# Moving the low half of x from POOL to DVE in the first stage of an attention and feed-forward kernel

## The chip, the cores and the metric

One core of one Trainium2 chip. The metric is the time of one execution on the device in microseconds, as the median of several runs. The kernel before takes 1428.94 us.

## What is computed

A layer with attention and a gated feed-forward part side by side, on x of 4 x 1024 x 512 in float32. The reference, cut to what matters:

```python
xn = (x - mean(x)) / sqrt(var(x) + 1e-5)
q, k, v = (heads(xn @ W.T) for W in (Wq, Wk, Wv))     # 16 heads of 32
scores = where(causal, q @ k.T / sqrt(32), lowest)
attn = softmax(scores) @ v
gate = silu((xn @ fp8(gate_w)) * gate_scale)
up = (xn @ fp8(up_w)) * up_scale
ffn = ((gate * up) @ fp8(down_w)) * down_scale
out = x + attn @ Wo.T + ffn
```

## The kernel before

The kernel has two stages. `prepare` normalises x, makes q, k and v and stores them to DRAM; `attend` does the attention and the feed-forward part and reads them back. Products are made in float16 with a high and a low part for each float32 operand: high x high, high x low, low x high.

`prepare` goes over x in eight tiles of 512 rows, t = 0 to 7. A tile has twelve chunks, c = 0 to 11: four of q, four of k, four of v. TensorE makes a chunk in twelve matmuls of 128x512 (L797) into one of four banks; ScalarE copies the high part out as float16 (L487 for q and k, L491 for v), DVE subtracts it from the bank for the low part (L695, L699), and SP stores the pair (L386, L396). TensorE may begin chunk c when DVE has made the low part of chunk c - 4, since they share a bank. The float16 pairs of q and k stand in four buffers, so ScalarE's high part of chunk c also waits until the store of chunk c - 4 has landed.

While the chunks of tile t go by, the engines also make ready tile t + 1, each at a fixed place in its own hand-written order. In tiles 2 to 6 that is:

- DVE: statistics of x behind chunk 0 (L512, L516), the factor 1/sqrt(var) behind chunk 1 (L522 to L530), `normalise` behind chunk 2 (L537, x_in to xn).
- ScalarE: `x_high` behind chunk 4 (L450): the high half of xn as float16, into `x_part`.
- POOL: `x_low` (L429): xn less its high half, 128x2048, into the low half of `x_part`. POOL waits for `x_high` and for TensorE to be done with the former low half. Tile 0 has its low half from DVE (`first_x_low`, L594) instead.
- TensorE: `turn_x` behind chunk 9: 32 transposes (L737), in four fills, two of the high and two of the low half.
- ScalarE and DVE: `copy_x` behind chunk 10 (L469, L588): the turned halves into `x_t`. TensorE begins the next tile when both are done.

DVE has one more duty: rounding a piece of the feed-forward weights to fp8 in float32, three times a tile (`round_weights`, L616 to L632: maximum, mask of the exponent into `cmag`, L622 which clips `cmag`, L624 which adds it to `raw`, and the last step). In tiles 2 to 5 the three stand behind chunks 4, 6 and 8, in tile 6 behind 4, 6 and 9. Tile 0 and tile 1 also bring in the weights Wk, Wv and Wo: `weights_low` (L578) makes a low part of 128x2048 on DVE, `turn_weights` turns them on TensorE, `copy_weights` (L455, L544) takes them out. Tile 0 rounds behind chunks 7, 8 and 9; tile 1 has `weights_low(3)` and a rounding behind chunk 5, then further ones behind 7 and 8. Tile 0 makes `x_high` behind chunk 7.

In tiles 6 and 7 TensorE also makes scores of the first heads (L171), for whose row maxima DVE reduces the banks (`row_maxima`, L194, L199) behind chunks 3 to 8. Turning x in tile 6 waits for the twelfth of these reductions.

SP issues, once DVE's low part of chunk 11 is there, in this order: the store of v (L396), three loads of feed-forward weights (L339, L342), two stores of turned x (L367), then the stores of q and k as they come. Where DVE's order is decided:

```python
first_tile = {..., 6: ("normalise",), 7: ("round 0",), 8: ("round 1",), 9: ("round 2",)}
second_tile = {0: ("statistics",), 1: ("factor",), 2: ("normalise", "max 3"), 4: ("power 3",),
               5: ("low 3", "round 0"), 7: ("round 1",), 8: ("round 2",)}
other_tile = {0: ("statistics",), 1: ("factor",), 2: ("normalise",), 4: ("round 0",),
              6: ("round 1",), 8: ("round 2",)}
```

Of the kernel before, what the change touches and what calls it, by code (L numbers as in the profile page):

```python
# [18 lines left out]
ALU = mybir.AluOpType  # L19
# [12 lines left out]
NT = B * S // TILE  # L32
# [4 lines left out]
HI, LO = 0, 1  # L37
# [97 lines left out]
def wait(eng, sem, value):  # L135

    if value > 0:
        eng.wait_ge(sem, value)
# [72 lines left out]
def low_maxima(nc, pool, rows, m, par):  # L211

    pool.wait_ge(rows.m_red, NM * (m + 1))
    nc.gpsimd.tensor_scalar(rows.m_neg[:, :], rows.mx[par][:, :], -1.0 / MSCALE, None, ALU.mult).then_inc(rows.m_neg_set, 1)
    pool.wait_ge(rows.m_neg_set, m + 1)
    pool.wait_ge(rows.m_hi, m + 1)
    nc.gpsimd.tensor_tensor(rows.m_part[:, 8:16], rows.m_neg[:, :], rows.m_part[:, 0:8],
                            ALU.subtract).then_inc(rows.m_lo, 1)
# [15 lines left out]
def prepare(nc, x, weights, ffn, scales, xn_dram, keep, rows, bank):  # L234
# [11 lines left out]
    with ExitStack() as ctx:  # L246
        def sb(name, shape, dt):
            return ctx.enter_context(nc.sbuf_tensor(name, shape, dt))

        def sem(name):  # L250
            return ctx.enter_context(nc.semaphore(name))
# [10 lines left out]
        xn = sb("xn", [P, NB, D], F32)  # L262
        x_part = sb("x_part", [P, 2, NB, D], F16)
# [38 lines left out]
        xhi_done = sem("xhi_done")  # L302
        xlo_done = sem("xlo_done")
        xt_mm = sem("xt_mm")
# [24 lines left out]
        def has_next(t):  # L329
            return t < NT - 1  # L330
# [78 lines left out]
        @block.gpsimd  # L409
        def _(pool):  # L410
            nc.gpsimd.memset(ones[:, :], 1.0).then_inc(ones_ready, 1)
            nc.gpsimd.memset(ident[:, :], 0.0).then_inc(ident_zero, 1)
            pool.wait_ge(ident_zero, 1)
            nc.gpsimd.affine_select(out=ident[:, :], in_=ident[:, :], compare_op=ALU.not_equal, fill=1.0, base=0,
                                    pattern=[[-1, P]], channel_multiplier=1).then_inc(ident_set, 1)
            nc.gpsimd.memset(v_st[:, :, :, 2 * DK:VE], 1.0).then_inc(ones_set, 1)
            nc.gpsimd.memset(rows.mask[:, :], 0.0).then_inc(mask_zero, 1)
            pool.wait_ge(mask_zero, 1)

            nc.gpsimd.affine_select(out=rows.mask[:, 512 - P:512], in_=rows.mask[:, 512 - P:512],  # L420
                                    compare_op=ALU.is_ge, fill=MASKED, base=0, pattern=[[-1, P]],
                                    channel_multiplier=1).then_inc(mask_set, 1)

            def x_low(t):

                pool.wait_ge(xhi_done, t + 1)

                wait(pool, xt_mm, 4 * t)
                nc.gpsimd.tensor_tensor(x_part[:, LO, :, :], xn[:, :, :], x_part[:, HI, :, :],  # L429
                                        ALU.subtract).then_inc(xlo_done, 1)  # L430

            for t in range(1, NT):
                x_low(t)
            low_maxima(nc, pool, rows, 0, 0)

        def wmax_bank(m):
# [66 lines left out]
        def _(dve):  # L503
# [63 lines left out]
            def weights_power(m):  # L567

                at = slice(m, m + 1)
                dve.wait_ge(wmax_mm, m + 1)  # L570
                nc.vector.tensor_reduce(w_max[:, at], wmax_bank(m), AX.X, ALU.max).then_inc(wpow_set, 1)
                dve.wait_ge(wpow_set, m + 1)
                nc.vector.tensor_copy(w_pow[:, at], w_max[:, at])
                nc.vector.reciprocal(w_inv[:, at], w_max[:, at]).then_inc(winv_done, 1)
# [14 lines left out]

            for k_rows in rows.k_st:  # L590
                nc.vector.memset(k_rows[3 * DK:3 * DK + 2, :], MSCALE).then_inc(k_ones_set, 1)
            def first_x_low():
                dve.wait_ge(xhi_done, 1)
                nc.vector.tensor_tensor(x_part[:, LO, :, :], xn[:, :, :], x_part[:, HI, :, :],  # L594
                                        ALU.subtract).then_inc(xlo_done, 1)

# [5 lines left out]
            copy_weights(0)  # L602
            normalise(0)
            weights_max(1)
            first_x_low()
            weights_power(1)
            copy_x(0, 0)

# [76 lines left out]
            def tile(t, par):  # L685
                plan = {0: first_tile, 1: second_tile, NT - 2: before_last, NT - 1: last_tile}.get(t, other_tile)
                for c in range(12):
                    for m in WEIGHTS_COPIED.get((t, c), ()):
                        copy_weights(m)
                    if t == c == 0:  # L690
                        weights_low(1)
                    dve.wait_ge(hi_done, 12 * t + c + 1)
                    src = bank[2 + c % 4][:, :]
                    if c < 8:
                        nc.vector.tensor_tensor(qk_st[c % 4][:, LO, :], src, qk_st[c % 4][:, HI, :],  # L695
                                                ALU.subtract).then_inc(lo_done, 1)
                    else:
                        at = v_st[:, :, c - 8, :]
                        nc.vector.tensor_tensor(at[:, :, 0:DK], src.rearrange("p (h d) -> p h d", d=DK),  # L699
                                                at[:, :, DK:2 * DK], ALU.subtract).then_inc(lo_done, 1)  # L700
                    for what in plan.get(c, ()):
                        name, _, m = what.partition(" ")
                        if name == "max":
                            weights_max(int(m))
                        elif name == "power":
                            weights_power(int(m))
                            if m == "3":
                                factors_of_weights()
                        elif name == "low":
                            weights_low(int(m))  # L710
                        elif name == "feed-forward":
                            feed_forward_factors()
                        elif name == "round":
                            round_weights(t, int(m))
                        elif has_next(t):
                            {"statistics": norm_statistics, "factor": norm_factor, "normalise": normalise}[name](t + 1)
                    if c == X_TURNED and has_next(t):
                        copy_x(t + 1, 1 - par)
                    if t >= NT - 2:
                        head = t - (NT - 2)  # L720
                        if head == 0 and c == min(EARLY_MAXIMA[0]):
                            dve.wait_ge(mask_set, 1)
                        row_maxima(nc, dve, rows, early_banks, head, head, EARLY_MAXIMA[head].get(c, ()))
                        if head == 1 and c == 1:
                            copy_row(nc, dve, rows, bank[7], 0, 0, 0)
# [725 lines left out]
```

## Time and profile before

| | us |
|---|---|
| median of three runs | 1428.94 (1428.7 to 1429.1) |
| profiled execution, its own time | 1425.56 |
| its span in the trace | 1423.8 |
| DVE busy | 1111.2 (78%) |
| POOL busy | 919.7 (65%) |
| POOL's L429, seven times | 29.0 |
| mean granted clock of TensorE | 0.988 |

The span is the time from the first to the last instruction of the profiled execution. Busy times are sums over one engine's instructions, and overlap between engines. The granted clock is the share of full speed that TensorE was given. Times inside the trace count from the start of the span. In a timeline a line stands for one or several merged instructions; "idle before" is the time that the engine stood still ahead of it, with what ended it.

### The profile page before, as it was taken

The numbers are of one execution on the slowest core, as the hardware profiler recorded it, in microseconds if no ns is written. First come the engines' busy times: TensorE is split into PE (matmuls) and PEld (weight loads), VectorE is DVE, ScalarE is ACT, GpSimd is POOL, SyncE is SP. The second block draws the span as 40 slices with busy tenths as digits, with TensorE's granted clock in tenths as the row PEclk, the third lists the DMA queues.
The fourth block names the chain that finished last, engine by engine and source line by source line (L and its number), as shares of the span: only waits on it lengthen the run. The fifth ranks groups of instructions, "written<-read, shape, count | busy, mean of one in ns | idle before, by whom it ended". The sixth has DMA issues, their size and how long they took to land.

```text
span 1423.8 us, 34052 instructions
## 1 busy us (share of the span) xinstructions
PE 1325.6 (93%) x12254; PEld 856.1 (60%) x12254; DVE 1111.2 (78%) x2982; ACT 945.0 (66%) x1790; POOL 919.7 (65%) x1171
## 2 busy tenths in 40 slices
PE   4878899988799999999999999999999999999987
PEld 2434444433566666666767676766767676766754
DVE  7868888887787887878787887878787887878763
ACT  3332222221788887888888787878888887878851
POOL 0100111110688888988888888888888888888862
PEclk9999999999899999999999999999999999999999
DMA  6454766624321211212121212212121212222121
GB/s 211 125 160 120 205 187 186 173 92 148 79 61 32 76 47 47 72 36 76 39 76 47 69 39 69 77 46 76 32 77 45 76 39 68 65 58 76 32 61 60
DMA packets 116410, 119.56 MB, mean 84 GB/s; under 512 B 27090, under 2 KB 84690, under 8 KB 116242
## 3 DMA queue, kind: packets, MB, share of 16 engines
q1 hardware_dynamic: 116242, 117.38, 28.5%
q8 instruction: 98, 1.61, 0.5%
q14 instruction: 70, 0.57, 0.1%
HBM read 74.86 MB, written 42.21 MB: 82 GB/s over the span
## 4 chain that ended last, share of the span: by engine, by line
PE 55%; DVE 11%; ACT 4%; issue 3%; POOL 1%; DMA 0%; SPq 0%; ACTq 0%; DVEq 0%
PE bank L1256 16%; PE bank L1270 12%; PE bank L1234 8%; PE bank L171 7%; PE bank L1221 7%; PE bank L1289 4%; DVE junk L194 2%; DVE probs L912 2%; ACT probs L1046 2%; DVE ga L1158 2%; DVE mx L199 1%; DVE fu L1163 1%; PE bank L1280 1%; ACT th L1053 1%; POOL probs L912 1%
## 5 line engine op out<-in xcount | busy, mean ns | idle before, releaser
L1076 ACT ACTIVATE p<-bank,s_exp 128x512 f32<-128x512 f32 x576 | 398.1, 691 | 184.3 <-PE bank L1221 179.5
L912 POOL TENSOR_TENSOR probs<-p,probs 128x512 f16<-128x512 f32 x448 | 519.8, 1171 | 0.0
L1046 ACT CAST probs<-p 128x512 f16<-128x512 f32 x576 | 353.9, 614 | 0.1
L1006 POOL TENSOR_SCALAR_AFFINE_SELECT p<-p 128x256 f32<-128x256 f32 (+1 forms) x320 | 152.2, 475 | 139.2 <-ACT p L1076 137.6
L171 PE MATMUL bank<-k_st,q_st 96*128 96x512 f16 (+3 forms) x792 | 221.8, 328 | 18.7 <-DVE mx L194 9.8
L199 DVE TENSOR_REDUCE mx<-bank 128x1 f32<-128x512 f32 x264 | 180.0, 685 | 65.6 <-PE bank L171 60.9
L1221 PE MATMUL bank<-q_st,k_st 98*128 98x512 f16 (+3 forms) x768 | 221.3, 329 | 7.5 <-DVE k_st L1166 5.7
L1234 PEld LDWEIGHTS bank<-v_sb,probs 128*128 128x128 f16 x4608 | 197.8, 97 | 50.2 <-issue 1.6
L1234 PE MATMUL bank<-v_sb,probs 128*128 128x65 f16 x4608 | 213.9, 192 | 2.6 <-DVE attn L1125 2.6
L1256 PE MATMUL bank<-xt,wg 128*128 128x256 f16 x1536 | 200.2, 273 | 5.2 <-DVE fu L1163 5.2
L1256 PE MATMUL bank<-xt,wu 128*128 128x256 f16 x1536 | 199.4, 273 | 0.0
L429 POOL TENSOR_TENSOR x_part<-xn,x_part 128x2048 f16<-128x2048 f32 x7 | 29.0, 4142 | 262.6 <-ACT x_part L450 262.6
L1270 PE MATMUL bank<-wd,fuse 128*128 128x512 f16 x768 | 190.6, 378 | 0.9 <-DVE ff_out L1151 0.9
L797 PE MATMUL bank<-x_t,w_t 128*128 128x512 f16 x768 | 176.4, 390 | 10.7 <-issue 9.7
L194 DVE CUSTOM_DVE_ANT_0 junk<-bank,mask,mx 128x128 bf16<-128x128 f32 (+3 forms) x264 | 143.3, 543 | 26.5 <-PE bank L171 26.0
L1256 PEld LDWEIGHTS bank<-xt,wg 128*128 128x128 f16 x1536 | 141.1, 98 | 33.7 <-DVE fu L1163 7.2
L1256 PEld LDWEIGHTS bank<-xt,wu 128*128 128x128 f16 x1536 | 142.0, 98 | 23.9 <-issue 0.2
L194 DVE CUSTOM_DVE_ANT_0 junk<-bank,mask 128x128 bf16<-128x128 f32 (+3 forms) x264 | 123.2, 486 | 32.8 <-PE bank L171 32.8
L993 POOL TENSOR_TENSOR fuse<-fu,fuse 128x256 f16<-128x256 f32 x192 | 137.5, 716 | 15.6 <-ACT fuse L1061 15.5
L797 PEld LDWEIGHTS bank<-x_t,w_t 128*128 128x128 f16 x768 | 75.9, 100 | 106.5 <-issue 21.4
L487 ACT CAST qk_st<-bank 128x512 f16<-128x512 f32 x64 | 37.3, 587 | 147.4 <-PE bank L797 122.9
L171 PEld LDWEIGHTS bank<-k_st,q_st 96*128 96x128 f16 x792 | 74.8, 98 | 98.3 <-DVE mx L194 29.5
(115 smaller groups left out, 1720.5 us busy)
## 6 DMA issues: line engine op xcount, KB each, us to landing
q_st<-q_parts SPq DMA_DIRECT2D x201, 64.0 KB, 2.0
k_st<-k_parts SPq DMA_DIRECT2D x201, 64.0 KB, 2.0
v_sb<-v_parts SPq DMA_DIRECT2D x66, 132.0 KB, 2.2
xt<-xn_parts SPq DMA_DIRECT2D x17, 512.0 KB, 4.5
v_parts<-v_st SPq DMA_DIRECT2D x8, 1056.0 KB, 7.5
x_in<-in_L_attn_x SPq DMA_DIRECT2D x8, 1024.0 KB, 6.3
xn_parts<-x_t SPq DMA_DIRECT2D x16, 512.0 KB, 7.8
q_parts<-qk_st SPq DMA_DIRECT2D x32, 256.0 KB, 4.1
```

The lines of the kernel that those rows point to most:

```text
L171: nc.tensor.matmul(banks[u % len(banks)][:, 0:w], rows.q_st[i][part, blk * P:(blk + 1) * P], rows.k_st[i][part, k0:k0 + w], start=True, st ...
L194: ins = nc.vector.tensor_tensor_reduce(out=rows.junk[u % 2][:, 0:w], in0=src, in1=rows.mask[:, 512 - w:512], scale=1.0, scalar=at if k0 el ...
L199: ins = nc.vector.tensor_reduce(at, src, AX.X, ALU.max)
L797: mm = nc.tensor.matmul(bank[2 + c % 4][:, :], lhs, rhs, start=first, stop=((wp, xp) == TERMS[-1] and kc == KC - 1))
L912: ops.tensor_tensor(probs[s % 2][:, LO, at], p32[k % RING][:, :], probs[s % 2][:, HI, at], ALU.subtract).then_inc(signal, 1)
L1006: nc.gpsimd.affine_select(out=at, in_=at, compare_op=ALU.is_ge, fill=0.0, base=0, pattern=[[0, blocks], [1, P]], channel_multiplier=-1).th ...
L1046: nc.scalar.copy(probs[s % 2][:, HI, u * 512:(u + 1) * 512], p32[k % RING][:, :]).then_inc(p_hi, 1)
L1076: nc.scalar.activation(p32[k % RING][:, :], st_bank[(s + u) % 2][:, :], ACT.Exp, scale=s_exp[:, :]).then_inc(exp_done, 1)
L1221: mm = nc.tensor.matmul(st_bank[(s + u) % 2][:, at:at + w], k_st[s][:, j * P:(j + 1) * P], q_st[s][:, q0:q0 + w], start=True, stop=True)
L1234: mm = nc.tensor.matmul(o_half[:, i % (QB // 2), :], probs[s % 2][:, part, at:at + P], v_sb[s][:, j, 0:VN], start=(j == 0 and part == HI), ...
L1256: mm = nc.tensor.matmul(ff_bank[f % 2][:, h * FT:(h + 1) * FT], (wg8, wu8)[h][:, kc, f * P:(f + 1) * P], xt[:, part, kc, :], start=(part = ...
L1270: mm = nc.tensor.matmul(misc[:, :], fuse[:, part, f, i * P:(i + 1) * P], wd8[:, f, :], start=(f == 0 and part == HI), stop=(f == FC - 1 an ...
```

## The change

POOL's `x_low` and its loop over tiles 1 to 7 are taken out. DVE's `first_x_low` becomes `x_low(t)`, with the two waits that POOL had, and is called for tile t + 1 behind what the plan has for chunk 8 (in tile 0) or for chunk 5 (in the others). The waits of `normalise` and of `turn_x` on the same counters stay.

```diff
@@ POOL, in prepare
-            def x_low(t):
-
-                pool.wait_ge(xhi_done, t + 1)
-
-                wait(pool, xt_mm, 4 * t)
-                nc.gpsimd.tensor_tensor(x_part[:, LO, :, :], xn[:, :, :], x_part[:, HI, :, :],
-                                        ALU.subtract).then_inc(xlo_done, 1)
-
-            for t in range(1, NT):
-                x_low(t)
             low_maxima(nc, pool, rows, 0, 0)
@@ DVE, in prepare
-            def first_x_low():
-                dve.wait_ge(xhi_done, 1)
+            def x_low(t):
+
+                dve.wait_ge(xhi_done, t + 1)
+
+                wait(dve, xt_mm, 4 * t)
                 nc.vector.tensor_tensor(x_part[:, LO, :, :], xn[:, :, :], x_part[:, HI, :, :],
                                         ALU.subtract).then_inc(xlo_done, 1)
...
-            first_x_low()
+            x_low(0)
...
+                    if c == (8 if t == 0 else 5) and has_next(t):
+                        x_low(t + 1)
                     if c == X_TURNED and has_next(t):
                         copy_x(t + 1, 1 - par)
```

In the changed kernel the lines of DVE in `prepare` stand 7 to 10 lower: L615 there is L622 here, L688 is L695, L692 is L699, L587 is L594.

DVE in tile 3, from chunk 4's low half to the middle of the second rounding. Before:

```order
L616 TENSOR_REDUCE ff_max<-raw 128x1
L619 TENSOR_SCALAR cmag<-raw 128x768
L622 TENSOR_SCALAR cmag<-cmag 128x768
L624 SCALAR_TENSOR_TENSOR raw<-cmag,raw 128x768
L629 SCALAR_TENSOR_TENSOR wg<-cmag,raw 128x768
L695 TENSOR_TENSOR qk_st<-bank,qk_st 128x512 x2
L616 TENSOR_REDUCE ff_max<-raw 128x1
```

And with the change:

```order
L609 TENSOR_REDUCE ff_max<-raw 128x1
L612 TENSOR_SCALAR cmag<-raw 128x768
L615 TENSOR_SCALAR cmag<-cmag 128x768
L617 SCALAR_TENSOR_TENSOR raw<-cmag,raw 128x768
L622 SCALAR_TENSOR_TENSOR wg<-cmag,raw 128x768
L688 TENSOR_TENSOR qk_st<-bank,qk_st 128x512
L587 TENSOR_TENSOR x_part<-xn,x_part 128x2048
L688 TENSOR_TENSOR qk_st<-bank,qk_st 128x512
L609 TENSOR_REDUCE ff_max<-raw 128x1
```

The low halves of chunks 5 and 6 stood together behind the first rounding; now x_low stands between them.

DVE in tile 0, from the end of the second rounding to the third, with the change (before, nothing stood between the rounding's last step and chunk 9's low half):

```order
L622 SCALAR_TENSOR_TENSOR wu<-cmag,raw 128x768
L587 TENSOR_TENSOR x_part<-xn,x_part 128x2048
L692 TENSOR_TENSOR v_st<-bank,v_st 128x16x32
L612 TENSOR_SCALAR cmag<-raw 128x768
L615 TENSOR_SCALAR cmag<-cmag 128x768
```

x_low for tile 1 is made ahead of chunk 9's low half, and everything behind it on DVE moves back by one instruction of 128x2048.

POOL, from the end of its start-up to its first work on maxima. Before:

```order
L417 MEMSET mask 128x512
L420 AFFINE_SELECT mask<-mask 128x128
L429 TENSOR_TENSOR x_part<-xn,x_part 128x2048 x7
L214 TENSOR_SCALAR m_neg<-mx 128x8
L217 TENSOR_TENSOR m_part<-m_neg,m_part 128x8
```

With the change the row of L429 is gone and the others stand as they were: POOL has nothing to do until the first head's maxima are reduced, in tile 6.

## Rows read from the trace of the kernel before

**Rows 1.** The page: busy time of each engine, share of the span, instructions.
```profile
PE 1325.6 (93%) x12254; PEld 856.1 (60%) x12254; DVE 1111.2 (78%) x2982; ACT 945.0 (66%) x1790; POOL 919.7 (65%) x1171
```
**Rows 2.** Timeline of PE, tile 3: start, duration, instructions, idle before and its releaser.
```profile
190.20 2.76 PE L797 MATMUL bank<-w_t,x_t 128*128 128x512 f16 x12 [1.66 <-DVE qk_st L695]
...
201.39 20.88 PE L797 MATMUL bank<-x_t,w_t 128*128 128x512 f16 x96 [1.46 <-issue]
```
**Rows 3.** Timeline of DVE, tile 3, from chunk 4's low half to chunk 11's.
```profile
181.20 0.69 DVE L695 TENSOR_TENSOR qk_st<-bank,qk_st 128x512 f16<-128x512 f32 x1 [2.70 <-ACT qk_st L487]
...
183.25 4.31 DVE L622 TENSOR_SCALAR cmag<-cmag 128x768 f32<-128x768 f32 x1
...
201.21 0.68 DVE L699 TENSOR_TENSOR v_st<-bank,v_st 128x512 f16<-128x512 f32 x1
```
**Rows 4.** Instructions on tile cmag, 120 to 345 us: ns min/median/max, first and last start.
```profile
L622 DVE TENSOR_SCALAR cmag<-cmag x18: 559/560/4308, 122.4 to 341.8; 128x768 f32<-128x768 f32 x18
L624 DVE SCALAR_TENSOR_TENSOR raw<-cmag,raw x18: 957/959/959, 122.9 to 342.4; 128x768 f32<-128x768 f32 x18
```
**Rows 5.** Timeline of POOL, the first L429 and that of tile 3.
```profile
61.35 4.43 POOL L429 TENSOR_TENSOR x_part<-xn,x_part 128x2048 f16<-128x2048 f32 x1 [58.65 <-ACT x_part L450]
...
183.04 4.10 POOL L429 TENSOR_TENSOR x_part<-xn,x_part 128x2048 f16<-128x2048 f32 x1 [32.22 <-ACT x_part L450]
```
**Rows 6.** Timeline of DVE, single instructions before and in tiles 0 and 1.
```profile
23.99 2.28 DVE L594 TENSOR_TENSOR x_part<-xn,x_part 128x2048 f16<-128x2048 f32 x1
...
46.47 2.34 DVE L578 SCALAR_TENSOR_TENSOR w_part<-w_raw,w_inv,w_part 128x2048 f16<-128x2048 f32 x1
...
61.89 4.70 DVE L624 SCALAR_TENSOR_TENSOR raw<-cmag,raw 128x768 f32<-128x768 f32 x1
...
105.93 5.11 DVE L578 SCALAR_TENSOR_TENSOR w_part<-w_raw,w_inv,w_part 128x2048 f16<-128x2048 f32 x1
```
**Rows 7.** Timeline of ACT, the high half of chunk 4 in tile 4.
```profile
215.97 0.59 ACT L487 CAST qk_st<-bank 128x512 f16<-128x512 f32 x1 [3.44 <-DMA q_parts<-qk_st]
```
**Rows 8.** Timeline of DVE, tile 0: the low halves of chunks 8, 9 and 10.
```profile
67.50 0.68 DVE L699 TENSOR_TENSOR v_st<-bank,v_st 128x512 f16<-128x512 f32 x1
...
72.01 0.69 DVE L699 TENSOR_TENSOR v_st<-bank,v_st 128x512 f16<-128x512 f32 x1
...
75.66 0.68 DVE L699 TENSOR_TENSOR v_st<-bank,v_st 128x512 f16<-128x512 f32 x1
```
**Rows 9.** Timeline of PE, turning x in tile 0 to the start of tile 1.
```profile
65.84 1.07 PE L737 MATMUL bank<-ident,x_part 128*128 128x128 f16 x16 [2.06 <-POOL x_part L429]
66.74 7.03 PE L797 MATMUL bank<-w_t,x_t 128*128 128x512 f16 x24
77.64 12.02 PE L797 MATMUL bank<-x_t,w_t 128*128 128x512 f16 x48 [3.87 <-issue]
```
**Rows 10.** Timeline of PE, tile 6 from its start to the start of tile 7.
```profile
272.94 10.52 PE L797 MATMUL bank<-x_t,w_t 128*128 128x512 f16 x48 [1.46 <-issue]
...
297.21 0.29 PE L171 MATMUL bank<-k_st,q_st 96*128 96x128 f16 x1 [5.00 <-DVE mx L194]
...
298.22 4.91 PE L797 MATMUL bank<-x_t,w_t 128*128 128x512 f16 x12
...
308.86 1.95 PE L737 MATMUL bank<-ident,x_part 128*128 128x128 f16 x32
...
316.04 2.75 PE L797 MATMUL bank<-x_t,w_t 128*128 128x512 f16 x12
```
**Rows 11.** PE by stretch: us, PE busy, granted clock, DMA share, GB/s.
```profile
66.91:71.05 4.14, 4.14 (x13) 0.59 0.00 0
...
148.60:157.00 8.40, 6.07 (x36) 1.00 0.68 210
```
**Rows 12.** Timeline of PE, tile 1: the last three fills of turned x.
```profile
121.35 1.50 PE L737 MATMUL bank<-ident,x_part 128*128 128x128 f16 x24 [1.90 <-issue]
```
**Rows 13.** Timeline of DVE, the twelfth reduction in tile 6.
```profile
307.85 0.75 DVE L194 CUSTOM_DVE_ANT_0 junk<-bank,mask,mx 128x512 bf16<-128x512 f32 x1
```

## The prediction

> **What bounds the kernel now.** I started with the busy time by engine [rows 1]: TensorE is busy for 93% of the span, so a gain has to show up as TensorE waiting less. The change touches only the first stage, `prepare`, some 350 us of 1423.8. So I read next what TensorE waits for there. In tile 3 (the pattern of tiles 2 to 5) it stops twice [rows 2]: 1.66 us before chunk 9, released by DVE's low half of chunk 5, and 1.46 us before the next tile's start at 201.39, put down to "issue". That second stop ends just after DVE's two copies of turned x, which lie right before DVE's last low half at 201.21 [rows 3]. Both stops point at DVE.
>
> In DVE's timeline of that tile [rows 3] the engine works without a gap from chunk 4's low half at 181.20 to chunk 11's, which ends at 201.89: 20.69 us. One row in it is odd: L622, on 128x768, takes 4.31 us, while the median of that line is 0.56 [rows 4]. POOL's x_low (L429) runs in those very microseconds, 183.04 to 187.14 [rows 5], and L622 ends at 187.56. In tile 0 another line is slow, L624 with 4.70 us against a median of 0.96, and L429 runs from 61.35 to 65.78; in tile 1 it is L578, 5.11 us against 2.34 in tile 0 [rows 4 to 6]. Three lines, seven tiles, always the DVE instruction that meets L429: DVE is held until POOL is through. So the idle time that POOL shows is no reason to keep x_low there: DVE pays for it, 3.75 us a tile (4.31 less 0.56).
>
> The other half of a tile's period is a transfer: ScalarE's high half of chunk 4 waits for the store of chunk 0, whose buffer it reuses, until 215.97 in tile 4 [rows 7]. SP issues the stores and loads of a new tile behind DVE's last low half of the old one, so this half starts from DVE too: 201.89 to 215.97 is 14.1 us. Period = this transfer time + 0.6 (high half) + DVE's chain. What shortens DVE's chain shortens the tile.
>
> **The change part by part.** *Removed:* seven L429 of 4.1 to 4.4 us on POOL [rows 5], and with them the hold on DVE. *Added:* seven subtractions of 128x2048 on DVE; the one that was there already takes 2.28 us [rows 6]; a successor that doesn't need its result starts some 0.08 before its end, as rows in DVE's timeline do, so 2.20. *Wait added on DVE:* for x_high of the next tile. ScalarE does it right after chunk 4's high half; DVE arrives after a whole rounding, so it waits for nothing. Queued behind x_low on DVE are the low halves from chunk 6 on (9 in tile 0), and for those wait TensorE's banks and its turning of x.
>
> *Tiles 2 to 5.* DVE's chain: -3.75 + 2.20 = **-1.55 us each, -6.2 in all**. The stop before chunk 9 goes, since chunk 5's low half now stands ahead of x_low and no longer behind a hold. x_low ends some 2 us before TensorE is ready to turn x. The stop before the next tile stays near 1.5 (2.5 in tile 2), so DVE still bounds, not TensorE.
>
> *Tile 0.* Here x_low stands behind chunk 8's rounding. Low half 8 moves from 67.50 [rows 8] to 63.76 (L624: -3.74). The next low half stood 4.51 behind it (72.01), so x_low runs from 68.27 to 70.55. TensorE had waited 2.06 for POOL until 65.84 [rows 9]; it now waits until 70.6, 4.76 later, 6.8 us in all. Chunks 10 and 11 follow; they took 7.03 us, against 5.3 for two at full clock (half of the 10.52 for four, rows 10), as the granted clock was 0.59 from 66.91 to 71.05 [rows 11], a mean of its levels 1.2 and 2.4 GHz. I take the same slow pair, since TensorE stands still for longer than it did. Chunk 10 then ends at 75.8 (71.05 + 4.76); with ScalarE's 0.59 and two hand-overs DVE's low half 10 moves from 75.66 [rows 8] to 76.6, and tile 1 starts at 78.58 in place of 77.64: +0.94. But the stop of 3.87 before tile 1 [rows 9] shrinks to nearly nothing. Its four chunks took 12.02 us behind that stop, 1.50 above 10.52, and this comes back. **Tile 0: -0.56.**
>
> *Tile 1.* L578 loses 2.76 (5.11 less 2.35), x_low adds 2.20, so DVE's copy of the turned weights comes 0.56 earlier. TensorE waits for that copy until 121.35 [rows 12]. But it comes to this wait sooner: it turns the weights 2.76 earlier and goes into the two chunks behind them at full clock. Before 121.35 it had stood idle 1.90 and ran on at full clock; now it stands idle about 5.6. Behind the stop of 5.00 in tile 6 the next chunk took 4.91 us where 2.6 is full clock [rows 10]. The slow stretches shown here cost 1.5, 1.7 and 2.3 us; I take 1.7, the one that also began with transposes. TensorE is the last to arrive there. **Tile 1: -0.56 + 1.70 = +1.14.**
>
> *Tile 6.* The first maxima of the scores are mixed in. TensorE stops 5.00 us for a reduction that stands behind the held L622, and the slow chunk follows [rows 10]. Without the hold the stop is 5.00 - 3.75 = 1.25 and the chunk runs at full clock: it ends near 297.1 instead of 303.1. Most of these 6 us aren't kept: turning x waits for the twelfth reduction, and that one stands behind x_low. It ends at 308.60 [rows 13] and moves by 1.55 and by 0.24 of waiting for ScalarE that goes, to 306.8; TensorE, which turned at 308.86, follows at 306.9. **Tile 6: -1.96.** Tile 7 has no x_low; it and the attention stage shift whole.
>
> *Free:* POOL gets no work, and its part of the maxima waits for DVE and ScalarE as before. ScalarE and SP keep their instructions and order.
>
> **Sum:** -0.56 + 1.14 - 6.20 - 1.96 = **-7.6 us**. The profiled execution took 1425.56 around its span of 1423.8, and would take 1418.0; the median of the runs, 1428.94, lies 3.4 above it, and I put the difference on it unchanged: 1428.94 - 7.6, to a rounding **1421.4 us**.
>
> **The rivals.**
> (A) *The clock does not fall* at the two new stops: 1.7 more in tile 0 and in tile 1, -11.0, 1418.0. Against it: stops of 5.00 and 3.87 us were each followed by a slow stretch [rows 9, 10]. For it: in 148.60 to 157.00 TensorE was idle for 8.40 - 6.07 = 2.33 us and stayed at full clock [rows 11]; so the length matters, and I know it by examples only. The Trainium skill ("TensorE: Matmul & The Clock Gate", What's actually happening) says that the number of slow matmuls varies from run to run of one kernel; no row here shows one stop twice. The reverse, two falls more (start of tile 1, tile 6), gives -4.4: 1424.5.
> (B) *The transfers bound the tile.* If the stores before chunk 4 take as much longer as DVE's chain gets shorter, tiles 2 to 5 give nothing and -1.4 is left: 1427.5, no change. For it: 14 us of a period are theirs [rows 7], with a DMA share of 0.68 in 148.60 to 157.00 [rows 11]. Against it: they are issued from DVE's last low half on, and at 0.68 the engines aren't full.
> (C) *DVE's hold isn't POOL's.* If L622 keeps its 4.31 (through its own operand, or loads into `raw`), x_low is pure load on the engine that bounds the tile: 2.20 in each of tiles 2 to 6, some 3.9 in tile 1 and 3.2 in tile 0 with their clock falls: +18, 1447. The point from which it decides is a rest of 1.55 us in L622: below it the change gains, above it loses. For it: the profile names no releaser there. Against it: three different lines, each only beside L429, and 0.56 without it. The Trainium skill ("Perfetto Trace Analysis", Optimizing Scalar/DVE Operations) advises the opposite move, work off a saturated DVE to ScalarE or even GpSimd, and adds that between DVE and GpSimd it might not help, as they share a port. By its first half this change would be slower, as in this rival; by its second, as forecast.
>
> **How the numbers follow.** Forecast, with its clock falls (1419.5 to 1423.3), 0.60; A 0.17; its reverse 0.13; B 0.07; C 0.03. The range leaves out B, C and the far ends of A: 1417.6 to 1424.8. A difference of 0.2% (2.9 us) is about what a measurement of this kernel can tell from none. Faster by more (under 1426.1): 0.90; within: 0.07, B; slower: 0.03, C.
>
> **What would show it.** L622 at 0.56 us in every tile, L624 of tile 0 at 0.96, L578 of tile 1 at 2.35; x_low on DVE at 2.3 us in eight tiles, with no idle time before it. From the start of tile 4 to that of tile 6 some 68.5 us instead of 71.55 (201.39 to 272.94, rows 2, 10). TensorE idle for about 6.8 us before the second half of tile 0's turning and 5.6 us in tile 1's last third, each with a slow stretch behind it. Tile 7 starting at about 308.4 in place of 316.04 [rows 10]. I am wrong if L622 stays above 1 us, if the way from low half 11 to chunk 4's high half grows past 15 us, or if x_low waits for ScalarE.

## The result, and the profile after

The changed kernel takes 1422.39 us (median of five runs, 1420.89 to 1423.64); the kernel before took 1429.1 beside it (five runs, 1428.7 to 1430.38). The ratio is 0.9948, with a 95% interval of 0.9934 to 0.9963: **6.7 us faster**, where -7.6 was forecast. Two later comparisons of the same two kernels gave the same 6.7 in medians (1425.16 to 1418.45, 1425.95 to 1419.27).

Busy time on the page of the changed kernel (columns as in [rows 1]):

```profile
span 1420.5 us, 34052 instructions
...
PE 1325.5 (93%) x12254; PEld 857.3 (60%) x12254; DVE 1101.5 (78%) x2989; ACT 943.8 (66%) x1790; POOL 890.1 (63%) x1164
```

DVE has seven instructions more and is busy 9.7 us less than in [rows 1]: it got 16.0 us of new subtractions (7 x 2.28) and lost 25.7. Of these, 25.2 are durations that had only been stretched, which counted as busy: 3.74 in one L624, 2.76 in one L578 and 3.75 in each of five L622. The numbers of the changed kernel's lines are lower than before; L615 is the former L622, L617 the former L624, L568 the former L578, L587 the subtraction, L688 and L692 the low halves of a chunk.

Instructions on two tiles of the changed kernel, over the whole span (columns as in [rows 4]):

```profile
L615 DVE TENSOR_SCALAR cmag<-cmag x24: 559/560/561, 61.2 to 343.9; 128x768 f32<-128x768 f32 x24
L617 DVE SCALAR_TENSOR_TENSOR raw<-cmag,raw x24: 957/959/960, 61.8 to 344.5; 128x768 f32<-128x768 f32 x24
...
L587 DVE TENSOR_TENSOR x_part<-xn,x_part x8: 2281/2282/2286, 23.6 to 290.1; 128x2048 f16<-128x2048 f32 x8
```

Every outlier of [rows 3, 4, 6] is gone (the four L568 take 9.4 us together, where the four L578 took 12.2), and the eight subtractions take the forecast 2.28 us. Timeline of DVE in tile 3 of the changed kernel, against [rows 3]:

```profile
180.48 0.69 DVE L688 TENSOR_TENSOR qk_st<-bank,qk_st 128x512 f16<-128x512 f32 x1 [2.28 <-ACT qk_st L477]
...
182.53 0.56 DVE L615 TENSOR_SCALAR cmag<-cmag 128x768 f32<-128x768 f32 x1
...
185.60 2.28 DVE L587 TENSOR_TENSOR x_part<-xn,x_part 128x2048 f16<-128x2048 f32 x1
...
198.94 0.68 DVE L692 TENSOR_TENSOR v_st<-bank,v_st 128x512 f16<-128x512 f32 x1
```

From chunk 4's low half to the end of chunk 11's DVE now works 19.14 us (180.48 to 199.62) in place of 20.69: 1.55 less, the term of the sum, and the subtraction has no idle time before it.

TensorE's timeline of the changed kernel shows the two stops that the change lengthens in tiles 0 and 1 (from 2.06 and 1.90), and the stop before tile 4; they answer to [rows 9], [rows 12] and [rows 2]:

```profile
70.50 1.89 PE L732 MATMUL bank<-ident,x_part 128*128 128x128 f16 x16 [6.84 <-DVE x_part L587]
72.18 6.24 PE L792 MATMUL bank<-w_t,x_t 128*128 128x512 f16 x24
...
120.51 2.72 PE L732 MATMUL bank<-ident,x_part 128*128 128x128 f16 x24 [5.77 <-issue]
123.02 6.42 PE L792 MATMUL bank<-w_t,x_t 128*128 128x512 f16 x24
...
199.13 20.88 PE L792 MATMUL bank<-x_t,w_t 128*128 128x512 f16 x96 [1.32 <-issue]
```

The stops are 6.84 and 5.77 us long (6.8 and 5.6 forecast), and behind both TensorE went slowly: the granted clock over these stretches of the changed kernel (stretch, us, busy and instructions, clock, DMA share, GB/s) was

```profile
70.50:72.18 1.68, 1.68 (x16) 0.50 0.00 0
...
120.51:123.02 2.51, 2.51 (x24) 0.50 0.03 7
123.02:129.40 6.38, 6.38 (x26) 0.83 0.00 0
```

0.50, the lower level of 1.2 GHz, through the transposes and into the pair of chunks behind them.

What an execution took apart, by TensorE's timeline. "Before 2", "changed 2" and "changed 3" are one more profile of the kernel before and two of the changed one, from the experiments below.

| start of, us | before | changed | before 2 | changed 2 | changed 3 |
|---|---|---|---|---|---|
| tile 0, chunk 8 | 57.55 | 57.42 | 58.09 | 58.12 | 57.01 |
| tile 1 | 77.64 | 78.48 | 78.18 | 79.33 | 77.75 |
| tile 2 | 128.09 | 129.50 | 129.07 | 130.48 | 128.53 |
| tile 6 | 272.94 | 268.69 | 273.85 | 270.17 | 266.44 |
| tile 7 | 316.04 | 310.73 | 316.97 | 311.98 | 307.40 |
| tile 7, chunk 8 | 341.63 | 338.61 | 344.84 | 337.84 | 332.99 |
| attention's first scores | 361.13 | 358.64 | 364.24 | 357.37 | 352.27 |
| span | 1423.8 | 1420.5 | 1427.6 | 1421.6 | 1415.3 |

Tile 7 starts 5.3 and 5.0 us earlier in the first two pairs, 9.1 in the last (against the mean of the two before; 0.8 of it lies ahead of chunk 8 of tile 0, where the change has touched nothing yet). The first profiled execution of the kernel before lay 3.4 us under its median of 1428.94, and the first pair of spans shows only -3.3. Most of the rest is in tile 7: its first eight chunks took 25.59 us there and 27.88 in the changed kernel, and 27.87 against 25.86 the other way round in the second pair. Both kernels show both lengths, so I don't put it down to the change. TensorE's timelines around chunk 7 of tile 7, the kernel before and the changed one:

```profile
337.83 0.28 PE L171 MATMUL bank<-k_st,q_st 96*128 96x256 f16 x1 [1.26 <-DVE mx L199]
...
338.66 2.75 PE L797 MATMUL bank<-x_t,w_t 128*128 128x512 f16 x12
```
```profile
333.48 0.40 PE L171 MATMUL bank<-k_st,q_st 96*128 96x256 f16 x1 [2.22 <-DVE mx L199]
...
334.48 3.91 PE L792 MATMUL bank<-x_t,w_t 128*128 128x512 f16 x12
```

Of the 2.29 us between them 0.96 is a longer stop and 1.16 a slower chunk behind it.

### The profile page after: what moved, and what is told of

The parts are those of the page before. It is cut to its first block, busy times and chain, and to the rows that moved or that the text cites. A ratio compares the mean times of both kernels' runs of the same rounds, so it can differ in the third digit from the quotient of the medians.

```text
span 1420.5 us, 34052 instructions
## 1 busy us (share of the span) xinstructions
PE 1325.5 (93%) x12254; PEld 857.3 (60%) x12254; DVE 1101.5 (78%) x2989; ACT 943.8 (66%) x1790; POOL 890.1 (63%) x1164
## 4 chain that ended last, share of the span: by engine, by line
PE 55%; DVE 11%; ACT 4%; issue 3%; POOL 1%; ACTq 0%; DVEq 0%
PE bank L1251 16%; PE bank L1265 12%; PE bank L1229 8%; PE bank L171 7%; PE bank L1216 7%; PE bank L1284 4%; DVE junk L194 2%; DVE probs L907 2%; ACT probs L1041 2%; DVE ga L1153 2%; DVE mx L199 2%; DVE fu L1158 1%; PE bank L1275 1%; ACT th L1048 1%; POOL probs L907 1%
## 5 line engine op out<-in xcount | busy, mean ns | idle before, releaser
L214 POOL TENSOR_SCALAR m_neg<-mx 128x8 f32<-128x8 f32 x65 | 15.8, 244 | 299.8 <-DVE mx L194 299.8
```

## The experiments

### Is it POOL that holds DVE, and does the hold last as long as POOL's instruction?

`before_2` and `after_2` are the kernel before and the changed one again, beside the two kernels that follow (kernel before there: 1425.16 us, median of 17 runs).

> The kernel before once more, for a second profile of it. Theory (the hold of DVE by POOL's x_low): L622 takes 4.31 us in tiles 2 to 6 again, L624 4.7 in tile 0, L578 5.1 in tile 1; time within 0.2% of the kernel before. The first profiled execution lay 3.4 us under the median of its runs: a second profile shows if that is in the first stage (clock falls) or behind it. If it is in the first stage, tile starts differ by single steps of 1 to 2 us; rival: they differ nowhere and the attention stage does by 3 us.

Measured: 1425.78 us, ratio 1.0008 (1.0 to 1.0017).

> The changed kernel once more. Time 0.995 of before (1420.9 to 1423.7 us). Theory: the start of tile 4 to that of tile 6 takes 68.5 to 69.6 us again (69.56 in its first profile), since DVE sets it; the places where TensorE's clock falls (tile 0, tile 1, tile 6, tile 7 in the first profile) may move by one or two, each worth 1 to 2.3 us. Rival (the transfers set what tiles 4 and 5 give): the same two tiles differ by more than 1 us between the profiles while DVE's rows are the same.

Measured: 1418.45 us, ratio 0.9959 (0.9947 to 0.9972).

`tiny_low_2` takes the work from POOL without giving it to DVE. POOL subtracts 8 elements of each partition only; the rest of x's low half is left out.

```diff
-                nc.gpsimd.tensor_tensor(x_part[:, LO, :, :], xn[:, :, :], x_part[:, HI, :, :],
+                nc.gpsimd.tensor_tensor(x_part[:, LO, 0, 0:8], xn[:, 0, 0:8], x_part[:, HI, 0, 0:8],
```

> The kernel before, but POOL's x_low takes 8 elements of each partition in place of 2048, so the low half of x is left as it was for tiles 1 to 7. It takes away the hold on DVE and adds no work to DVE. Theory (hold): L622 0.56 us in every tile, DVE's chain 3.75 us shorter a tile; tiles 2 to 5 then meet TensorE's own work at about 33.1 us a tile, so 12 us there, 3.8 in tile 0, 2.8 in tile 1, 3.8 in tile 6: -22 us against the kernel before, 1407. Rival (L622 is held by something else): L622 keeps 4.3 us and the time is within 0.2% of before. Rival (transfers set the tile): L622 0.56 us but tiles 2 to 5 stay at 35 to 37 us, -10 us.

Measured: 1404.31 us, ratio 0.9855 (0.9841 to 0.9869), 20.9 us less (22 expected). Tile cmag and TensorE's timeline of this kernel:

```profile
L622 DVE TENSOR_SCALAR cmag<-cmag x24: 559/560/561, 60.7 to 326.7; 128x768 f32<-128x768 f32 x24
```
```profile
183.09 5.34 PE L797 MATMUL bank<-w_t,x_t 128*128 128x512 f16 x24
188.48 11.81 PE L797 MATMUL bank<-x_t,w_t 128*128 128x512 f16 x54
```

L622 is at 0.56 in all 24. Tiles start every 33.1 us (155.41 to 254.68 for three) and TensorE passes into the next one with no idle time. So the hold is gone with POOL's long instruction, and the transfers fit into 33.1 us too: rival B falls.

`both_low_2` is the changed kernel in which POOL makes the same subtraction as well, into room that is free by then (that of the weights Wq), and nobody reads it; DVE's `normalise` waits for it, as it must before it overwrites xn.

```diff
+            for t in range(1, NT):
+                pool.wait_ge(xhi_done, t + 1)
+                nc.gpsimd.tensor_tensor(w_raw[0][:, :, 0:D // 2].bitcast(F16), xn[:, :, :], x_part[:, HI, :, :],
+                                        ALU.subtract).then_inc(xspare_done, 1)
...
+                wait(dve, xspare_done, t - 1)
```

> The changed kernel, and POOL makes the same subtraction once more at the place it had before, into the room of Wq, which is free by then; nothing reads it. DVE has the new work and the hold. Theory (hold): L615 (the former L622) takes 4.3 us again, L617 4.7 in tile 0, L568 5.1 in tile 1; 2.2 us more than the kernel before in each of tiles 2 to 6 and 3 to 4 in tiles 0 and 1: +14 to +18 us, 1443 to 1447. Rival (the hold comes from something other than POOL's work): as the changed kernel, 1422.

Measured: 1446.18 us, ratio 1.0144 (1.013 to 1.0158), 21.0 us over the kernel before, where 14 to 18 were expected. Tiles 2 to 5 cost 8.5 us more than in the kernel before (153.3 in place of 144.85, 2.1 each, as expected), tile 6 1.9; tile 0 costs 4.9 and tile 1 3.8, more than expected. Its timelines in tile 3, first of POOL, then of DVE:

```profile
193.91 4.10 POOL L427 TENSOR_TENSOR w_raw<-xn,x_part 128x2048 f16<-128x2048 f32 x1 [33.74 <-ACT x_part L445]
```
```profile
193.53 0.55 DVE L618 TENSOR_SCALAR cmag<-raw 128x768 uint32<-128x768 uint32 x1
194.12 4.31 DVE L621 TENSOR_SCALAR cmag<-cmag 128x768 f32<-128x768 f32 x1
198.46 0.96 DVE L623 SCALAR_TENSOR_TENSOR raw<-cmag,raw 128x768 f32<-128x768 f32 x1
```

The 4.31 is back, in the instruction that began 0.21 after POOL's and ended 0.42 after it. The output of POOL's work has no reader here, so L621 doesn't wait for data. Rival C falls: what it feared, both the hold and the new work on DVE, comes only when POOL's instruction is kept, and the change takes it away. That 1446 lies near rival C's 1447 is chance in part: it is 21.0 over the kernel before beside it, where C had 18. The Trainium skill ("SBUF — State Buffer", SBUF: two separate sides) calls the port pair that DVE and GpSimd share an exclusive lock, kept for the whole instruction by whichever starts first. The trace agrees: 0.56 became 4.31 beside a POOL instruction of 4.10.

### One instruction at a time: four pieces on POOL

If the hold lasts one POOL instruction, shorter ones should hold DVE for less. `pool_in_four` is the kernel before, with POOL's subtraction in four of 128x512.

```diff
-                nc.gpsimd.tensor_tensor(x_part[:, LO, :, :], xn[:, :, :], x_part[:, HI, :, :],
-                                        ALU.subtract).then_inc(xlo_done, 1)
+                for i in range(NB):
+                    last = nc.gpsimd.tensor_tensor(x_part[:, LO, i, :], xn[:, i, :], x_part[:, HI, i, :],
+                                                   ALU.subtract)
+                last.then_inc(xlo_done, 1)
```

> The kernel before, with POOL's x_low as four instructions of 128x512 in place of one of 128x2048; nothing else changed. It asks how long a hold lasts: for one POOL instruction, or while POOL has such work. Theory (DVE is held for the one instruction that it meets): no DVE row is longer than about 2.1 us (one piece of about 1.1 and its own time), L622, L624 and L629 are held one piece each, some 2.9 us a tile in place of 3.75, and L429's last piece ends later; 3 to 6 us faster than before. Rival (the hold lasts until POOL has no more of it): L622 4.3 to 4.8 us, time within 0.2% of before. In both the changed kernel stays faster.

Measured: 1417.9 us, ratio 0.9951 (0.9939 to 0.9963), beside a kernel before at 1425.12 (ten runs; so for the next three). Its timelines of POOL and DVE in tile 3:

```profile
180.56 6.28 POOL L430 TENSOR_TENSOR x_part<-xn,x_part 128x512 f16<-128x512 f32 x4 [28.32 <-ACT x_part L452]
```
```profile
180.77 1.40 DVE L624 TENSOR_SCALAR cmag<-cmag 128x768 f32<-128x768 f32 x1
182.20 1.79 DVE L626 SCALAR_TENSOR_TENSOR raw<-cmag,raw 128x768 f32<-128x768 f32 x1
184.03 1.80 DVE L631 SCALAR_TENSOR_TENSOR wg<-cmag,raw 128x768 f16<-128x768 f32 x1
```

Three DVE instructions are held for 0.84, 0.83 and 0.84 (over 0.56, 0.96 and 0.96), 2.5 in all in place of 3.75, and POOL's work takes 6.28 in place of 4.10: the two engines now take turns, and POOL waits too: its four pieces of tile 3 take 1.18, 1.46, 1.87 and 1.87 us. With the work still on POOL this is **as fast as the changed kernel** (ratio 0.9951, against 0.9948, 0.9959 and 0.9957), 7.2 us under the kernel before, where I had expected 3 to 6 and the changed kernel to stay ahead. DVE pays 2.5 here and 2.20 there; the 0.3 a tile can't be told apart in the medians.

### The stops that the change makes in tiles 0 and 1

`early_tile0` puts tile 0's subtraction behind chunk 7 and so ahead of two roundings.

```diff
-                    if c == (8 if t == 0 else 5) and has_next(t):
+                    if c == (7 if t == 0 else 5) and has_next(t):
```

> The changed kernel, with tile 0's x_low one chunk earlier on DVE (behind chunk 7's rounding in place of chunk 8's). Theory (of my sum, tile 0: TensorE's stop of 6.8 us behind it delays tile 1): TensorE's stop before the second half of turning is about 2.2 us as before the change, tile 1 starts 2.4 us earlier than in the changed kernel (76.1 in place of 78.5); of this 1.5 is lost if the clock falls at tile 1's start. 1 to 2.5 us faster than the changed kernel, 8 to 9 under the kernel before. Rival (tile 0's place doesn't matter, DVE's chain does it): same as the changed kernel.

Measured: 1420.31 us, ratio 0.9962 (0.9949 to 0.9976). TensorE's timeline of tile 0:

```profile
66.71 1.07 PE L732 MATMUL bank<-ident,x_part 128*128 128x128 f16 x16 [2.33 <-DVE x_part L587]
67.62 5.34 PE L792 MATMUL bank<-w_t,x_t 128*128 128x512 f16 x24
76.71 11.82 PE L792 MATMUL bank<-x_t,w_t 128*128 128x512 f16 x48 [3.75 <-issue]
```

The stop of 6.84 is down to 2.33 and the pair runs at full clock, but a stop of 3.75 comes ahead of tile 1 and a slow start behind it (48 matmuls in 11.82, against 10.52). Tile 1 starts 2.5 us earlier against chunk 8 of tile 0 (18.57 after it, 21.06 in the changed kernel), and tile 2 only 1.9: 70.16 after it against 72.08. The median shows none of it (4.8 us under the kernel before, where 8 to 9 were expected): the changed kernel itself had ratios of 0.9948, 0.9959 and 0.9957. Inconclusive.

`turn_first_tile1` moves tile 1's second rounding from behind chunk 7 to behind chunk 8, and its third from 8 to 9. In the changed kernel the second rounding stands ahead of DVE's copy of the turned weights, and TensorE stops 5.77 us for that copy.

```diff
-                           5: ("low 3", "round 0"), 7: ("round 1",), 8: ("round 2",)}
+                           5: ("low 3", "round 0"), 8: ("round 1",), 9: ("round 2",)}
```

> The changed kernel, with tile 1's second and third rounding one chunk or more later on DVE (behind chunks 8 and 9 in place of 7 and 8), so that the copy of the turned weights doesn't stand behind the second. Theory (of my sum, tile 1: TensorE's stop of 5.8 us and the slow clock behind it cost what x_low's side gains): the stop falls to about 1.8 us, the transposes behind it take 1.5 us in place of 2.7 and chunks 10 and 11 5.3 in place of 6.4; tile 1 to tile 2 takes 48 us in place of 51.1; 3 us faster than the changed kernel, 9 to 10 under the kernel before. Rival (DVE bounds tile 1 whatever the order): within 1 us of the changed kernel.

Measured: 1414.33 us, ratio 0.9921 (0.9907 to 0.9934). TensorE's timeline of tile 1:

```profile
116.00 1.50 PE L732 MATMUL bank<-ident,x_part 128*128 128x128 f16 x24 [1.86 <-issue]
117.34 5.34 PE L792 MATMUL bank<-w_t,x_t 128*128 128x512 f16 x24
125.96 20.88 PE L792 MATMUL bank<-x_t,w_t 128*128 128x512 f16 x96 [3.27 <-issue]
```

With the stop at 1.86 the transposes take 1.50 and the pair 5.34, all at full clock, where the changed kernel needed 2.72 and 6.42: this is what the slow stretch of tile 1 costs, 1.22 + 1.08 = 2.3 us. Tile 1 takes 47.96 in place of 51.02.

`three_places` has both edits, and tile 6's second and third roundings behind chunks 9 and 11, so that no rounding stands ahead of a reduction for which TensorE waits.

```diff
-                           6: ("round 1",), 9: ("round 2",)}
+                           9: ("round 1",), 11: ("round 2",)}
```

> Both of these, and in tile 6 the second and third rounding behind chunks 9 and 11 in place of 6 and 9, so that the reductions for which TensorE stops don't stand behind a rounding. Theory: tile 6 loses its stop of 1.8 us and the slow chunk behind it (4.2 to 4.4 us in place of 2.75); tile 7 starts 5 us earlier relative to tile 6's start, of which 2 to 3 are left at chunk 4 of tile 7, as the third rounding holds back SP's loads. With the other two 6 to 8 us faster than the changed kernel: 1411 to 1413 where that takes 1418.5, 13 to 15 under the kernel before. Rival (what tile 6 gains is waited for in tile 7, at the store of chunk 0): 4 to 5 us faster than the changed kernel.

Measured: **1410.74 us**, ratio 0.9899 (0.9885 to 0.9914), 14.4 us under the kernel before and the fastest of all that compute the whole. Tile 6 takes 37.79 us (264.87 to 302.66) in place of 42.04 (40.96 in the profile of the changed kernel in which the clock didn't fall); its stop of 1.79 ahead of chunk 9 and the slow chunk behind it are gone. The start of tile 2 gave a surprise. Timeline of TensorE, and its clock in that stretch:

```profile
125.74 23.62 PE L792 MATMUL bank<-x_t,w_t 128*128 128x512 f16 x96 [3.27 <-issue]
```
```profile
125.74:131.00 5.26, 5.26 (x13) 0.50 0.70 188
```

The stop is 3.27 us as in `turn_first_tile1`, where the same 96 matmuls ran at full clock in 20.88. Behind a stop of the same length they took 2.7 us more in this profile and nothing more in the other. By the start of tile 3, 1.2 us of it are left (35.82 after the start of tile 2, against 34.61), as the stop there is gone.

### Where there is a gap: an earlier place for the subtraction

DVE waits some 2.3 us for chunk 4's high half (the first line of tile 3 above). `low_in_gap` puts ScalarE's `x_high` and DVE's `x_low` into that time in tiles 2 to 6, behind chunk 3. It was run with a third pair of profiles (kernel before: 1425.95 us, eleven runs).

```diff
-                    if c == (7 if t == 0 else 4) and has_next(t):
+                    if c == (7 if t == 0 else 4 if t == 1 else 3) and has_next(t):
...
-                    if c == (8 if t == 0 else 5) and has_next(t):
+                    if c == (8 if t == 0 else 5 if t == 1 else 3) and has_next(t):
```

> The changed kernel, beside the next three on one chip, to compare them. 0.995 to 0.996 of the kernel before.

Measured: 1419.27 us, ratio 0.9957 (0.9942 to 0.9972).

> The changed kernel, with x_high on ScalarE and x_low on DVE one and two chunks earlier in tiles 2 to 6, both behind chunk 3: there both engines wait for the store of chunk 0 (DVE some 3 us before chunk 4's low half). Theory (DVE's chain from chunk 4's low half on sets the tile): x_low runs mostly in that wait; chunk 4's low half comes at most 0.9 us later, the chain behind it is 2.2 shorter: 1.3 us a tile, starts of tiles 2 to 6 some 33.2 to 34 apart in place of 34.8 on the mean, near TensorE's own 33.05; 5 to 6.5 us faster than the changed kernel, 11 to 12 under before. Rival (the transfers set the tile): no more than 1 us faster than the changed kernel, and the wait for chunk 0's store as long as before.

Measured: 1415.86 us, ratio 0.9927 (0.9915 to 0.9939), 3.4 us under `after_3`, less than the 5 to 6.5 expected. Tiles 2 to 5 came as expected: 133.73 us for the four in place of 137.91, with stops of only 0.40. Tile 6 gained nothing (41.06 in place of 40.96). Timelines of ScalarE and of TensorE in this kernel:

```profile
212.73 1.22 ACT L477 CAST qk_st<-bank 128x512 f16<-128x512 f32 x2 [0.35 <-DMA q_parts<-qk_st]
```
```profile
197.62 2.75 PE L792 MATMUL bank<-x_t,w_t 128*128 128x512 f16 x12 [0.41 <-issue]
```

ScalarE waits 0.35 to 1.49 for the stores, where [rows 7] has 3.44: the transfers are nearly, and not quite, hidden.

`pool_in_gap` asks the same of the kernel before: `x_high` one chunk earlier in tiles 2 to 6, the subtraction still one instruction on POOL.

```diff
-                    if c == (7 if t == 0 else 4) and has_next(t):
+                    if c == (7 if t == 0 else 4 if t == 1 else 3) and has_next(t):
```

> The kernel before, x_low on POOL in one instruction as it was, with only x_high one chunk earlier in tiles 2 to 6 (behind chunk 3). It moves POOL's 4.1 us so that more than half of it falls into DVE's wait for chunk 4 and on rows that POOL doesn't hold (chunk 4's low half, which reads a bank, and the reduction L616). Theory (only a DVE instruction that meets POOL's is held, and for what is left of it): the row that is held is L619 and not L622, for 1.2 to 1.6 us in place of 3.75; 2.2 to 2.5 us a tile in tiles 2 to 6: 10 to 12 us faster than the kernel before, and so faster than the changed kernel. Rival (the work has to leave POOL): within 2 us of the kernel before.

Measured: 1416.56 us, ratio 0.993 (0.9917 to 0.9943). Its timelines of POOL and DVE in tile 3:

```profile
177.94 4.07 POOL L429 TENSOR_TENSOR x_part<-xn,x_part 128x2048 f16<-128x2048 f32 x1 [29.67 <-ACT x_part L450]
```
```profile
179.31 0.69 DVE L695 TENSOR_TENSOR qk_st<-bank,qk_st 128x512 f16<-128x512 f32 x1 [2.78 <-ACT qk_st L487]
179.92 0.94 DVE L616 TENSOR_REDUCE ff_max<-raw 128x1 f32<-128x768 f32 x1
180.78 1.65 DVE L619 TENSOR_SCALAR cmag<-raw 128x768 uint32<-128x768 uint32 x1
182.46 0.56 DVE L622 TENSOR_SCALAR cmag<-cmag 128x768 f32<-128x768 f32 x1
```

POOL's 4.07 us now lie mostly on time in which DVE waited anyway. The low half L695 and the reduction L616 run beside POOL and aren't held; L619, the next instruction, is held for the rest of POOL's work, 1.1 us instead of 3.75. How much is left of that work depends on when chunk 4's high half comes and DVE can start: over tiles 2 to 6 L619 takes 1.22, 1.65, 2.35, 2.11 and 2.58 us, so it is held for 0.7 to 2.0, 1.4 on the mean. The kernel is 9.4 us faster than the kernel before (10 to 12 expected). **One moved line of the kernel before does as well as the change or better** (0.993 against 0.9957; the intervals just touch).

`four_places` joins `three_places` and `low_in_gap`.

> The version with three places moved, and x_high and x_low of tiles 2 to 6 behind chunk 3. Theory: the two gains add: 5 to 6 us faster than the version with three places, 0.985 to 0.987 of before. Rival: tiles 2 to 5 are at TensorE's own length either way, 0.990 as before it.

Measured: 1413.1 us, ratio 0.991 (0.9897 to 0.9924). The gains don't add. Its profile has tiles 3 to 5 at 33.4 us each, but tile 2 at 35.95, and slow stretches of TensorE in four places (the starts of tiles 1 and 2 with 13.09 for 48 and 23.66 for 96 matmuls, a chunk of 4.13 in tile 6 and one of 4.44 in tile 7). The first two lie ahead of the shorter tiles and come in `three_places` too (12.21 and 23.62); for the other two I can't say whether the shorter tiles bring them on or whether this profile had bad luck.

## Why the prediction was right, point by point

- **What bounds the kernel.** Right. The outlying durations on DVE are POOL's hold: they are gone in the changed kernel and in `tiny_low_2`, are back in `both_low_2`, and in `pool_in_gap` shorten to what is left of POOL's instruction when DVE meets it.
- **Tiles 2 to 5, forecast -6.2.** Measured -5.7 (144.85 to 139.19), -5.1 (144.78 to 139.69) and, in the third profile of the changed kernel (137.91), -6.9. From chunk 4's high half to the end of chunk 11's low half each of the four tiles took 21.31 us before and takes 19.75 or 19.76 in the changed kernel: DVE's chain lost 1.55 in each, as forecast. The rest lies in the other half of the period. Timeline of ScalarE in the changed kernel, the high half of chunk 4 in tile 4, against [rows 7]:

```profile
214.49 0.58 ACT L477 CAST qk_st<-bank 128x512 f16<-128x512 f32 x1 [4.22 <-DMA q_parts<-qk_st]
```

From the end of the low half of chunk 11 (199.62) this is 14.87 us where it was 14.08. Over tiles 2 to 5 the four stretches of this kind add up to 59.4 us, 0.55 more than the 58.8 before, and with -6.2 that gives the -5.7 measured. In the third profile they are 57.9, 0.9 less: they scatter, and a small part of rival B's price is in the first profile. In the second a slow stretch of TensorE adds to them: 96 matmuls in 22.57 us at the start of tile 3 lengthen DVE's chain there by 0.6. My sign for being wrong, "past 15 us", came true (15.17 in tile 5) although the forecast held: it was badly chosen, as the kernel before already had 15.01 in one tile. From tile 4 to tile 6 it took 69.56, against 71.55 before and 68.5 forecast.

- **Tile 0, forecast -0.56.** Right, size and shape. Tile 1 starts 0.97 later against chunk 8 of tile 0 (+0.94 forecast), the stop before tile 1 is gone and its first 48 matmuls take 10.52 in place of 12.02. The rows that the term was read from were this execution's, though: the second profile of the kernel before had the same stop in tile 0 (2.05) with a fast pair behind it,

```profile
67.28 5.34 PE L797 MATMUL bank<-w_t,x_t 128*128 128x512 f16 x24
78.18 12.32 PE L797 MATMUL bank<-x_t,w_t 128*128 128x512 f16 x48 [5.56 <-issue]
```

and then a stop of 5.56 instead of 3.87 [rows 9], so that tile 1 starts 20.09 after chunk 8 in both. The slow start behind that stop cost 1.80 there.

- **Tile 1, forecast +1.14.** Right sign, too small: **the term for the slow stretch was mis-sized**. I took 1.7 us from the three examples of 1.5, 1.7 and 2.3; it is 2.3, by the transposes and the pair with and without the fall. The stop ended 1.68 earlier against the start of the tile, where 1.50 + 0.56 = 2.06 was due: 0.38 less, lost ahead of chunk 4, whose low half came only 1.13 earlier. From its start to that of tile 2, tile 1 took 51.02 us in place of 50.45, 0.93 more than forecast.
- **Tile 6, forecast -1.96.** Measured -1.06 and -1.31, and -2.14 in the third profile (40.96 for the tile, 43.10 before). The stop that was 5.00 [rows 10] is 1.09 (1.25 forecast). But a stop of 1.79, which the prediction didn't have, lies two chunks on, and in two profiles of three the clock fell behind it. Timelines of TensorE, the changed kernel and its third profile:

```profile
298.44 0.34 PE L171 MATMUL bank<-k_st,q_st 96*128 96x384 f16 x1 [1.79 <-DVE mx L194]
...
299.27 4.44 PE L792 MATMUL bank<-w_t,x_t 128*128 128x512 f16 x12
```
```profile
296.20 0.34 PE L171 MATMUL bank<-k_st,q_st 96*128 96x384 f16 x1 [1.79 <-DVE mx L194]
...
297.03 2.75 PE L792 MATMUL bank<-w_t,x_t 128*128 128x512 f16 x12
```

A granted clock of 0.60 in the one and 1.00 in the other, behind the same stop. Without the fall the term was right within 0.2; the fall was in rival A's reverse (two falls more, at the start of tile 1 and in tile 6), and one of its two came.

- **The sum.** Start of tile 7 in place of 316.04: 308.4 forecast, 310.73, 311.98 and 307.40 measured. The median's 6.7 lies 0.9 from the forecast's 7.6. What is short of the forecast lies in tile 1 in all three profiles and in tiles 2 to 6 in two of them; in the third these gave more than forecast. Each term has its sign and its order of size; what is off is a slow clock, or the transfers ahead of chunk 4. That the medians come so near is luck in part, since single executions of one kernel differ by more than 0.9.
- **The rivals.** A (no falls in tiles 0 and 1): fell, both came in all three profiles of the changed kernel. B: fell in size (`tiny_low_2` reaches a tile of 33.1 us), though the transfers gave back 0.6 us in the first profile. C fell, as L615 is at 0.56 in the changed kernel, and `both_low_2` shows whose the hold is. Of the Trainium skill's advice ("Perfetto Trace Analysis", Optimizing Scalar/DVE Operations) its second half, that offloading between DVE and GpSimd might not help, was what counted here. The Trainium skill ("TensorE: Matmul & The Clock Gate", What's actually happening) says that the number of slow matmuls varies from run to run of one kernel. The page speaks of a kernel's start; the traces agree in its middle too, where 12 matmuls behind the same stop of 1.79 took 4.44, 4.24 and 2.75 us in three profiles of the changed kernel.

What stays open: which stops bring the clock down. Equal stops of 1.79, 2.05 and 3.27 us went either way, so I can't forecast single falls. The runs of one kernel differ by 7 us (1415.76 to 1423.04 for the changed kernel in the third comparison), and the mean granted clock goes with them (0.989 in the shortest, 0.983 in the longest), so the falls are likely a part of it. Not tried: `pool_in_gap` or `pool_in_four` together with the moved roundings of `three_places`.

## What to carry to other kernels

Look among the instructions of one line for durations that stick out and have no releaser: a POOL instruction beside them may be holding DVE, and then POOL's work is not free, whatever its idle time says. Before such work is moved to the busier engine, see whether it can be cut into shorter instructions or put where DVE waits anyway, and count each way by what DVE pays: 3.75 us held, 2.5 in four pieces, 2.2 on DVE itself, 0.7 to 2.0 in the gap. Follow where TensorE stops after the change: most of what was gained on top of it (14.4 us instead of 6.7) came from moving long work out from ahead of what TensorE waits for.

## What the runs showed of the hardware that was not expected

- Not every DVE instruction is held. Beside POOL's subtraction, TENSOR_SCALAR on float32 and uint32 in SBUF (L622, L619) and SCALAR_TENSOR_TENSOR with two SBUF inputs (L624, L578) waited; in `pool_in_gap` the TENSOR_REDUCE L616 took its usual 0.94 and L695, a TENSOR_TENSOR with one of its inputs in a bank, its usual 0.69.
- The hold works both ways: in four pieces POOL's subtraction takes 6.28 us in place of 4.10. The shortest piece takes 1.15 us, so by my estimate some 1.7 of the 6.28 are waits for DVE's instructions; the longest of the 28 pieces, 3.21, met the L580 of tile 1, a DVE instruction of 2.35 us when nothing holds it.
- TensorE's clock falls behind some stops and not behind others of the same length, in executions of one kernel too: a stop of 1.79 us was followed by chunks of 4.44, 4.24 and 2.75 us, one of 2.06 and 2.05 by 7.03 and 5.34 for 24 matmuls, and in two kernels that are alike in this tile one of 3.27 by 20.88 and by 23.62 us for 96.
